# A three-layer pairwise-product kernel: x tiles laid out in DRAM as SBUF holds them, loaded by transfers of 128 rows

## The reference

```python
h = x                                     # x: [512, 39, 16]
for i, S in enumerate([128, 128, 128]):
    Wr = Ws[i].reshape(39, h.shape[1], S)
    out = relu(einsum('bfd,bgd,fgs->bsd', x, h, Wr) + bs[i][None, :, None])
    if i != 2:
        h, direct = out[:, :64], out[:, 64:]
    else:
        direct = out
    outs.append(direct)
return sum(concatenate(outs, axis=1), axis=-1)      # [512, 256]
```

## Time and profile before

| what | us |
|---|---|
| median of 3 runs | 615.74 |
| lowest, highest | 610.09, 615.98 |
| the profiled execution | 616.65 |
| its span in the trace | 614.9 |
| PE busy | 566.6 (92%) |
| DVE busy | 533.9 (87%) |
| POOL busy | 517.8 (84%) |
| ACT busy | 376.7 (61%) |

### The profile page before, as it was taken

How to read it: one execution, slowest core, us unless ns; L and a number is a source line. 1 busy time by engine, 2 the same in 40 slices (tenths; PEclk the granted TensorE clock), 3 DMA queues, 4 the chain that set the end, 5 groups by cost and what they waited for, 6 DMA issues and landing times.

```text
span 614.9 us, 8379 instructions
## 1 busy us (share of the span) xinstructions
PE 566.6 (92%) x2032; PEld 386.3 (63%) x2032; DVE 533.9 (87%) x514; ACT 376.7 (61%) x421; POOL 517.8 (84%) x231
## 2 busy tenths in 40 slices
PE   0564679999999999999999999999999999999997
PEld 0332446667676667667676766767666766677665
DVE  2433588889998989999999999999999999999975
ACT  1422375747676675857676675756676675767653
POOL 0344479698998989898998989898989989898995
PEclk9895769999999999999999999999999999999999
DMA  8999999989998999999999999999998999986001
GB/s 205 214 207 212 215 199 228 205 203 191 225 205 210 217 199 215 192 223 196 227 207 221 213 202 226 204 226 181 224 199 212 207 203 225 206 194 150 0 3 34
DMA packets 33073, 118.76 MB, mean 193 GB/s; under 512 B 6817, under 2 KB 6945, under 8 KB 30928
## 3 DMA queue, kind: packets, MB, share of 16 engines
q1 hardware_dynamic: 33056, 118.57, 88.0%
HBM read 118.02 MB, written 0.52 MB: 193 GB/s over the span
## 4 chain that ended last, share of the span: by engine, by line
PE 79%; DMA 7%; issue 5%; POOL 4%; SPq 2%; DVE 1%; ACT 1%; POOLq 0%; ACTq 0%; DVEq 0%
PE acc L470 79%; DMA xwide<-x 5%; POOL z_lo L224 4%; DMA xshift<-x 2%; SPq L251 1%; DVE z_raw L353 1%; ACT z_hi L537 0%; SPq L240 0%; DVE z_whole L353 0%; SPq L234 0%; ACT h L540 0%; ACT last L540 0%; DVE z_lo L224 0%; ACT direct L540 0%; DVE z_hi L222 0%
## 5 line engine op out<-in xcount | busy, mean ns | idle before, releaser
L224 POOL TENSOR_TENSOR z_lo<-z_raw,z_hi 128x1024 fp32r<-128x1024 f32 (+2 forms) x224 | 511.9, 2324 | 82.2 <-ACT z_hi L537 80.2
L537 ACT CAST z_hi<-z_raw 128x1024 fp32r<-128x1024 f32 (+2 forms) x224 | 226.0, 1018 | 159.2 <-DVE z_raw L353 139.1
L353 DVE TENSOR_TENSOR z_raw<-h,xwide 128x1024 f32<-128x1024 f32 x192 | 230.5, 1218 | 26.7 <-ACT h L540 12.8
L470 PE MATMUL acc<-z_hi,w_hi 128*128 128x512 f32 (+2 forms) x560 | 223.4, 468 | 11.1 <-ACT z_hi L537 10.3
L470 PE MATMUL acc<-z_hi,w_lo 128*128 128x512 f32 (+2 forms) x560 | 184.1, 399 | 0.0
L470 PE MATMUL acc<-z_lo,w_hi 128*128 128x512 f32 (+1 forms) x528 | 173.8, 403 | 11.0 <-POOL z_lo L224 5.2
L470 PEld LDWEIGHTS acc<-z_hi,w_hi 128*128 128x128 f32 (+2 forms) x560 | 106.2, 191 | 74.7 <-issue 51.1
L470 PEld LDWEIGHTS acc<-z_lo,w_hi 128*128 128x128 f32 (+1 forms) x528 | 99.1, 190 | 41.0 <-POOL z_lo L224 11.1
L470 PEld LDWEIGHTS acc<-z_hi,w_lo 128*128 128x128 f32 (+2 forms) x560 | 106.4, 190 | 28.8 <-issue 3.8
L470 PE MATMUL acc<-z_whole,w_whole 128*128 128x512 f32 x256 | 121.7, 598 | 0.0
L470 PE MATMUL acc<-z_whole,w 117*128 117x512 f32 x128 | 65.0, 632 | 22.9 <-DVE z_whole L353 22.9
(11 more groups left out here) (16 smaller groups left out, 90.3 us busy)
## 6 DMA issues: line engine op xcount, KB each, us to landing
xwide<-x SPq DMA_DIRECT2D x320, 256.0 KB, 13.8
xshift<-x SPq DMA_DIRECT2D x45, 546.0 KB
xrep<-x SPq DMA_DIRECT2D x48, 78.0 KB
xwide<-w SPq DMA_DIRECT2D x2, 1024.0 KB, 24.8
xshift<-x SPq DMA_DIRECT2D x3, 312.0 KB
xshift<-x SPq DMA_DIRECT2D x3, 234.0 KB
w_whole<-w_rest SPq DMA_DIRECT2D x1, 512.0 KB, 19.5
w<-w0a SPq DMA_DIRECT2D x1, 409.5 KB
```

The source lines that it names most:

```text
L224: return eng.tensor_tensor(lo[0:rows, 0:n, :], z[0:rows, 0:n, :], hi[0:rows, 0:n, :].bitcast(F32), ALU.subtract)
L353: nc.vector.tensor_tensor(dst, in0, in1, ALU.mult).then_inc(made[kind], 1)
L470: return nc.tensor.matmul(dst, w[0:rows, PLACE[layer, t], :], z[0:rows, t - G * g, :], start=first and t == 0, stop=final and t == TILES[l ...
L537: nc.scalar.copy(z_hi[0:rows, slot("PV", pair, par, pos, HI_RING), 0:n, :], src).then_inc(hi_made, 1)
```

## The change

x is now built on the host in the forms that SBUF holds. `x` has, for each block and wide group, 128 rows of 4 KB: one row for each SBUF row, so a field stands 64 times in DRAM. `x0` has for each block 128 rows of 16 KB: slot 0 is what `xrep` held, slots 1 to 7 what `xshift` held, rows 117 to 127 are zero. `xrep` and `xshift` become one SBUF tile `xfirst` [128, 8, 512].

`load_wide` is one transfer of 128 rows (512 KB) with one increment of 16, where it was two of 64 rows. `load_first` is one transfer of 128 rows (2,048 KB), where `load_rep` and `load_shift` were six of 39 rows (1,872 KB in all). For block 0 it comes in two parts, the head (slots 0 to 4, 1,280 KB) and the rest. `copy_xrep` now waits for that whole transfer (for block 0, for the head), since `xrep` has no transfer of its own. Products, splits, matmuls, the schedule, and the places in SP's queue where x is loaded are as before.

```diff
-        xrep = sb("xrep", [P0, N])
-        xshift = sb("xshift", [P0, T0, N])
+        xfirst = sb("xfirst", [128, 1 + T0, N])
+        xshift = xfirst[0:P0, 1:1 + T0, :]
...
-            def load_rep(j):
-                for a in range(PER):
-                    src = bass.AP(x2.tensor, x2.offset + ROWS2 * N * j, [[N, FIELDS], [1, N]])
-                    sp.dma_start(xrep[a * FIELDS:(a + 1) * FIELDS, :], src).then_inc(xrep_in, 16)
-
-            def load_shift(j, landed, ts=range(T0)):
-                for a in range(PER):
-                    src = bass.AP(x2.tensor, x2.offset + ROWS2 * N * j + N * (T0 * a + ts[0]),
-                                  [[N, FIELDS], [1, len(ts) * N]])
-                    sp.dma_start(xshift[a * FIELDS:(a + 1) * FIELDS, ts[0]:ts[-1] + 1, :], src).then_inc(landed, 16)
+            def load_first(j, landed, slots=range(1 + T0)):
+                src = bass.AP(x0.tensor, x0.offset + 128 * (1 + T0) * N * j + N * slots[0],
+                              [[(1 + T0) * N, 128], [1, len(slots) * N]])
+                sp.dma_start(xfirst[:, slots[0]:slots[-1] + 1, :], src).then_inc(landed, 16)
 
             def load_wide(j, half, g):
-                for e in range(2):
-                    first = T12 * e + G * g
-                    if (g, e) != (G12 - 1, 1):
-                        run = [[1, G * N]]
-                    else:
-
-                        run = [[(FIELDS + T12 - 1 - first) * N, G], [1, N]]
-                    src = bass.AP(x2.tensor, x2.offset + ROWS2 * N * j + N * first, [[0, HALF]] + run)
-                    sp.dma_start(xwide[HALF * e:HALF * (e + 1), half, G * g:G * (g + 1), :],
-                                 src).then_inc(xw_in[half][g], 16)
+                src = bass.AP(x.tensor, x.offset + 128 * T12 * N * j + 128 * G * N * g, [[G * N, 128], [1, G * N]])
+                sp.dma_start(xwide[:, half, G * g:G * (g + 1), :], src).then_inc(xw_in[half][g], 16)
...
-                act.wait_ge(xrep_in, 16 * PER * (j + 2))
+                if isinstance(j, int) and j == -1:
+                    act.wait_ge(xfirst_head_in, 16)
+                else:
+                    act.wait_ge(xfirst_in, 16 * (j + 2))
...
-                nc.scalar.copy(xrep_psum[0:P0, :], xrep[:, :]).then_inc(xrep_ready, 1)
+                nc.scalar.copy(xrep_psum[0:P0, :], xfirst[0:P0, 0, :]).then_inc(xrep_ready, 1)
```

In the host part `x2` gives way to these two:

```diff
+    x0 = np.zeros((BLOCKS, 128, 1 + T0, N), np.float32)
+    for a in range(PER):
+        x0[:, FIELDS * a:FIELDS * (a + 1), 0] = x
+        for t in range(T0):
+            x0[:, FIELDS * a:FIELDS * (a + 1), 1 + t] = x[:, (f + T0 * a + t) % FIELDS]
...
-        "x2": np.concatenate([x, x], axis=1),
+        "x": np.repeat(x[:, pairs].reshape(BLOCKS, G12, G, 2, N).transpose(0, 1, 3, 2, 4), HALF, axis=2),
+        "x0": x0,
```

More of the change, by code:

```diff
@@ L21 @@
 BB = N // DIM
-ROWS2 = 2 * FIELDS
 SHIFTS = FIELDS // 2 + 1
@@ L123, with cin @@
 assert len(SPLIT0) > 0 and SPLIT_COUNT[1] <= 16 and SPLIT_COUNT[2] <= 16
-def cin(nc, x2, w0a, w0b, w1, w2, w_rest, b, out):
+def cin(nc, x, x0, w0a, w0b, w1, w2, w_rest, b, out):
     with ExitStack() as ctx:
@@ L171, in cin @@
         bias_in = sem("bias_in")
-        xrep_in = sem("xrep_in")
-        xshift_in = sem("xshift_in")
-        xshift_first_in = sem("xshift_first_in")
+        xfirst_in = sem("xfirst_in")
+        xfirst_head_in = sem("xfirst_head_in")
         xw_in = [[sem(f"xw_in{p}_{g}") for g in range(G12)] for p in range(2)]
@@ L260, in refill @@
                         sp.wait_ge(*made_all(j, 0))
-                        load_rep(j + 2)
-                        load_shift(j + 2, xshift_in)
+                        load_first(j + 2, xfirst_in)
                     if layer == 2 and not (isinstance(j, int) and j + 1 >= BLOCKS):
@@ L269, in _ @@
             sp.dma_start(w0t, w0b).then_inc(w0_in, 16)
-            load_rep(0)
-            load_shift(0, xshift_first_in, range(0, 2 * G))
-            load_shift(0, xshift_in, range(2 * G, T0))
+            load_first(0, xfirst_head_in, range(0, 1 + 2 * G))
+            load_first(0, xfirst_in, range(1 + 2 * G, 1 + T0))
             sp.dma_start(bias[:], b).then_inc(bias_in, 16)
@@ L279, in _ @@
             sp.wait_ge(*made_all(-1, 0))
-            load_rep(1)
-            load_shift(1, xshift_in)
+            load_first(1, xfirst_in)
             sp.dma_start(stage[2][:, 0:SPLIT_COUNT[2], :], w2).then_inc(w_staged[2], 16)
@@ L288, in _ @@
             sp.wait_ge(*made_all(0, 0))
-            load_rep(2)
-            load_shift(2, xshift_in)
+            load_first(2, xfirst_in)
             sp.wait_ge(w1_lo_made, 1)
@@ L323, in products @@
                     if first and g == 0:
-                        dve.wait_ge(xshift_first_in, 16 * PER)
+                        dve.wait_ge(xfirst_head_in, 16)
                     elif g == (2 if first else 0):
-                        dve.wait_ge(xshift_in, 16 * PER * (j + 2))
+                        dve.wait_ge(xfirst_in, 16 * (j + 2))
                     in0 = xrep_psum[0:P0, None, :].to_broadcast([P0, n, N])
@@ L331, in products @@
                         dve.wait_ge(h_ready[0], 2 * (j + 1))
-                    dve.wait_ge(xw_in[1 - par][g], 32 * (pair + par + 1))
+                    dve.wait_ge(xw_in[1 - par][g], 16 * (pair + par + 1))
                     in0 = h[0][:, None, :].to_broadcast([128, n, N])
@@ L649 @@
             w0b[s // T0, :, s % T0] = w0[g, f]
+    pairs = [(t, T12 + t if t < T12 - 1 else t) for t in range(T12)]
     def tiled(w):
         w = w.reshape(FIELDS, HALF, SIZE)
-        pairs = [(t, T12 + t if t < T12 - 1 else t) for t in range(T12)]
         return w[pairs].reshape(T12, 128, SIZE).transpose(1, 0, 2)
```

## The result

The changed kernel takes 590.15 us (median of 4 runs, 589.6 to 590.97), the kernel before 615.26 in the same comparison. The ratio is 0.961 with a 95% interval of 0.956 to 0.966. Predicted were 591.0 us and a range of 584 to 600. The kernel before scatters over about 1% (610.09 to 616.65 us over all its executions), so by medians the gain is 25.1 us here and 21.9 us in a later comparison (612.31 and 590.37).

What follows compares the result with a forecast made beforehand. PE bounds the steady part and DMA the start. Step 1 starting 24.7 us earlier cuts the span from 614.9 to 590.2 us; with 1.75 around it 591.9, less 0.9 for the median: 591.0 us, range 584 to 600.

Steps and rivals of the forecast that it cites:

- PE bounds the steady part: From 300 to 500 us PE is always busy, 34.1 us a step; a faster transfer is worth nothing there.
- The time is the start of step 1 plus 531.9 us: Whole span: PE's unbroken work began at 82.97 us, 531.9 us follow; only the first part can move.
- The rate: DMA in the start: transfers of 128 rows move at 380 GB/s instead of about 212.
- Step -1 and the start of step 0: First product at 9.8 us instead of 13.12; first layer-1 product on DVE at 18.8 instead of 25.68.
- Step 0: Block 1's layer-0 product at 29.8 us instead of 51.58, after a DMA wait; group 6 at 33.3 instead of 57.89.
- POOL is late next: Before block 1's h: POOL's w2 split, 4.56 us, ends at 40.2; h at 47.6 us instead of 72.28.
- Step 1's unbroken work: On PE: begins at 58.3 us instead of 82.97, a shift of 24.7 us.
- The copy's longer wait: On ACT in the steady part: about 13 products between issue and copy, some 15 us, cover it.
- The rate near 300: In the start: DMA rises only to about 300 GB/s, shift 18 us, 597 us; chance 0.15.
- Rival 2: In the start: rate 420 GB/s or more and PE at full clock, shift 28 to 30, 586 to 587 us; chance 0.15.
- Rival 3: Reading x from DRAM limits DMA, so the rate does not rise or falls: 628 us or 640; chance 0.05.
- Rival 4: PE's clock comes back later: 3.6 us more in step 1, another 1 before it, 596 us; chance 0.10.

Runs made afterwards that it cites:

- two halves: Changed kernel with each wide transfer split into two of 64 adjacent rows, each row with its own source row; 597.72 us, ratio 0.977.
- the even and odd rows: Changed kernel with each wide transfer split into two of 64 rows, one for even and one for odd rows; 590.27 us, ratio 0.963.
- the run with both edits: Changed kernel plus extra matmuls in PE's idle times and the low part of w2 made by DVE instead of POOL; 586.46 us, ratio 0.957.

## Why the prediction was right, step by step

- **PE bounds the steady part, and the change is worth nothing there.** Right: 371 matmuls in 100 us at a DMA share of 0.61, and 370 at 0.83 with two halves.
- **The time is the start of step 1 plus 531.9 us.** Right in form, 2.1 us too much. From 57.96 on 529.8 us pass. In the kernel before, late wide groups still held DVE up after 100 us, which I had not looked for. Its waits from 100 to 560 us (total, times, longest):

```profile
DVE z_raw L353 <- DMA xwide<-x: 6.1, 6, 2.0
...
PE acc L470 <- POOL z_lo L224: 0.9, 3, 0.4
```

  After the change neither line is there. The starts of the same matmuls in the two traces say where the 2.1 us come from. The lead of 25.0 us has grown to 25.6 at 86.56 (60.97 in the changed kernel), since the granted clock came back from 0.50 some 1.1 us sooner after step 1's start; to 26.8 at 165.09 (138.31), across two of the three waits for POOL's low parts; and to 27.1 at 268.30 (241.22). Whether the late wide groups caused those waits was not followed. That nobody waits for DMA in the steady part was read from 300 to 500 us and stretched over the first steps.
- **The rate.** 380 GB/s was predicted, 410 to 422 measured. The one short window at 393 was a better guide than the caution beside it. The attribution, rows of SBUF and not of DRAM, was right as far as the changed kernel goes; the form of the Trainium skill's rule (page "SBUF — State Buffer", section "Door 1: The DMA port swizzle": adjacent rows below 64 reach half of the ports) is borne out by the halves against the even and odd rows, as far as rates go; no view of the trace shows ports. Its 328 GB/s for 128 rows, which is given for single transfers of 1 MiB, was too low for a queue that is kept full.
- **Step -1 and the start of step 0.** First product: 9.8 predicted, 10.40 measured. First product of step 0: 18.8 predicted, 21.05 measured, and this is the mis-sized term. 0.6 of it is the late first product. For the rest, I had PE done at 17.4, 0.4 us behind POOL's second low part, but `relu0` began at 19.69. PE works in order: when POOL's first low part is there, PE still has nine matmuls to do, the two of that part (at 16.55), four of the next whole group and three of the last group. From 16.55 to `relu0` this took 3.1 us; for step 0 I had counted such a row of nine, here I had left it out. That PE's first four matmuls lasted 3.75 us, twice the 1.88 of later ones (at a granted clock of 1.00 in both places), is not the reason: in the run with both edits they lasted 2.06, and `relu0` came only 0.24 us earlier.
- **Step 0.** Layer-0 product 29.8, measured 29.66, but not for the reason given. At 415 GB/s the layer-0 x is there at about 27 (9.75 MB / 0.415 + 3.5, an estimate); ACT's copy began at 29.03 straight behind the high part of the last layer-1 group, which was late with the start of the step. A faster transfer and a later start, each by about 2 us, cancelled. Group 6 at 31.93, not 33.3, and with no wait for DMA.
- **POOL is late next.** w2's split 35.6 to 40.2, measured 35.54 to 40.14; group 7's low part was used by PE at 42.53 (42.6). h of block 1 at 47.6, measured 47.07. Right in place and time, but incomplete as a cause: with the split taken off POOL only 1.2 us were gained, since PE, which had run at the half clock from 23 to 29 us, was as late. From group 7's low part to `relu0` PE took 3.2 us, where I had taken 3.6.
- **Step 1's unbroken work** at 58.3, measured 57.96. **The copy's longer wait** on ACT was the 3.41 us before the first product, as worked out; the 1.73 us at 29.66 were ACT's queue, and no copy of a later block stands among DVE's waits.
- **The rivals.** The rate near 300 (597 us) did not come in the changed kernel, but it is what the halves gave: the sum for a lower rate was sound. Rival 2's rate, nearly 420 GB/s, came true, its 586 us did not. Its h at 43.9 came at 47.0: POOL's chain stood 2.4 us later (group 7's low part at 42.5, not 40.1), since step 0 had started late, and the nine matmuls took 3.2 us, not 2.4, although the clock of that stretch was 1.00. With the clock held throughout and POOL relieved, 586.46 us were measured. Rival 3, DRAM as the limit, is excluded by the changed kernel itself, which reads 128 different rows at 415 GB/s. Rival 4, a later return of the clock in step 1, went the other way: it came back sooner and gave 0.6 us.
- **How close the number is.** That it lies less than 1 us from the median is in part luck. In the traces the gain is 27.1 us and 24.7 was predicted, while the median that it was taken from, 615.74, is the highest of the kernel before (the others are 612.31 to 615.26). From 612.31 the same 24.7 us would have given 587.6, 2.5 us too little, still inside the range.

## What to carry to other kernels

When DMA, DVE, POOL and PE all look full, find the stretch in which the end of a wait is a DMA; here it was the first 80 us, and 25.0 of the 27.1 us that a doubled transfer rate gained are what it brought forward the first full step. Judge a transfer by the rows of SBUF it writes and by the form of its source: 64 adjacent rows ran at half rate, 64 alternate rows at full rate, pieces of 39 rows slower than the halves, 128 rows from a source of 16 runs at 265 to 297 GB/s, and an outermost count of 2 at an eighth. Add the parts of such a change with care: 12 and 15 us alone gave 22 together, for behind the transfers the next engines are waiting to become the limit.

## What the runs showed of the hardware that I had not expected

- 128 rows that all read the same 4 KB of DRAM move at 408 to 423 GB/s, no slower than 128 different runs.
- Transfers of 64 alternate rows of SBUF move at 414 to 422 GB/s, of 64 adjacent ones at about half (203 and 213 in the kernel before).
- A source of 16 runs, each read for 8 rows, fills all 128 rows and keeps the engines' mean share at 1.03 to 1.05, but moves only 265 to 297 GB/s in a mixed queue, like the adjacent halves.
- TensorE's clock fell to 1.2 GHz at 17 us in a kernel whose PE had been given extra work from 7.2 us on, and stayed up in two others with nearly the same work, one of which had the same idle time of 1.19 us before 17 us. What decides this is not shown. Whoever adds matmuls to hold the clock should look at the granted clock of each run before counting on them.
